# Rows of maxima of items 1, 3 and 4 sent through DRAM earlier on the sync queue, in a Trainium2 kernel of two layers

## What is computed

```python
x = L0_attn_u                                   # (1, 2048, 128)
x = x + _L0_attn_ref(_layernorm(x), ...)        # mixer
x = x + _L0_ffn_ref(_layernorm(x), ...)         # attention, experts
x = x + _L1_attn_ref(_layernorm(x), ...)        # selective scan
x = x + _L1_ffn_ref(_layernorm(x), ...)         # network
```

```python
scores = jnp.einsum('bqhd,bkhd->bhqk', q, k) / jnp.sqrt(jnp.float32(HEAD_DIM))
causal = jnp.tril(jnp.ones((S, S), bool))
scores = jnp.where(causal, scores, jnp.finfo(scores.dtype).min)
attn = jax.nn.softmax(scores, axis=-1)
out = jnp.einsum('bhqk,bkhd->bqhd', attn, v).reshape(B, S, D)
```

## Time and profile before

| | us |
|---|---|
| three runs | 1247.94, 1248.20, 1252.96 |
| median | 1248.2 |
| the profiled execution | 1252.22 |
| its span in the trace | 1249.9 |

### The profile page before, as it was taken

The page is one execution under the profiler, slowest core; times in us unless marked ns, Lnnn a source line. Parts: engine busy times, 40 slices in busy tenths (PEclk is TensorE's granted clock), DMA queues, the critical chain, the costliest instruction groups (busy, mean ns, idle before and its releaser), DMA issues.

```text
span 1249.9 us, 16003 instructions
## 1 busy us (share of the span) xinstructions
PE 1120.0 (90%) x5702; PEld 594.1 (48%) x5702; DVE 931.8 (75%) x1737; ACT 783.9 (63%) x1156; POOL 327.6 (26%) x271
## 2 busy tenths in 40 slices
PE   5889878888999999989999899999979789799998
PEld 2455554443333333333322288887633334357776
DVE  4788678857887888878864188887789999984432
ACT  4767632455655656656678898667758677455554
POOL 4233332210000000000012131210179788840000
PEclk9789889999998999999999999999989999899999
DMA  5211464345000000000000132211223222200000
GB/s 152 79 41 69 122 148 102 86 102 119 2 1 1 2 1 2 1 1 1 2 19 12 42 109 66 78 51 36 84 84 111 85 110 93 102 1 6 4 9 18
DMA packets 30623, 67.29 MB, mean 54 GB/s; under 512 B 3952, under 2 KB 16240, under 8 KB 28496
## 3 DMA queue, kind: packets, MB, share of 16 engines
q1 hardware_dynamic: 30544, 66.27, 18.5%
HBM read 57.47 MB, written 8.78 MB: 53 GB/s over the span
## 4 chain that ended last, share of the span: by engine, by line
PE 57%; DVE 14%; POOL 9%; issue 8%; ACT 7%; DMA 1%; SPq 0%; DVEq 0%; POOLq 0%; ACTq 0%
PE psum L1353 8%; PE psum L1238 8%; PE psum L405 7%; PE psum L407 7%; PE psum L406 7%; PE psum L1307 7%; POOL drive L2142 6%; DVE mx L1250 6%; DVE hst L2164 2%; ACT probs L1321 2%; PE psum L551 1%; PE psum L543 1%; PE psum L475 1%; PE psum L1956 1%; DMA m_rows<-mrow 1%
## 5 line engine op out<-in xcount | busy, mean ns | idle before, releaser
L1250 DVE TENSOR_REDUCE mx<-psum 128x1 f32<-128x512 f32 (+3 forms) x640 | 349.2, 603 | 64.8 <-PE psum L1238 35.2
L1321 ACT ACTIVATE probs<-psum 128x1024 f32<-128x1024 f32 (+1 forms) x320 | 283.6, 936 | 173.7 <-PE psum L1307 152.7
L1238 PE MATMUL psum<-kz,qa 128*128 128x512 bf16 (+3 forms) x640 | 199.3, 354 | 18.5 <-DVE mx L1250 12.8
L1307 PE MATMUL psum<-qa,kz 128*128 128x512 bf16 (+1 forms) x640 | 176.2, 363 | 7.8 <-DMA qa<-m_rows 4.4
L2142 POOL TENSOR_TENSOR drive<-du,b_bc 128x1024 f32<-128x1024 f32 x64 | 149.5, 2367 | 10.6 <-DVE hx_lo L675 9.1
L1353 PE MATMUL psum<-probs,v 128*32 128x512 f32 (+3 forms) x1280 | 150.8, 541 | 1.5 <-POOL probs L1332 1.4
L1238 PEld LDWEIGHTS psum<-kz,qa 128*128 128x128 bf16 x640 | 57.2, 97 | 180.5 <-DVE mx L1250 131.9
L2083 PE MATMUL psum<-hst,ident 128*128 128x512 f32 x256 | 120.3, 614 | 22.7 <-DVE u L2182 14.1
L1332 POOL TENSOR_SCALAR_AFFINE_SELECT probs<-probs 128x512 f32<-128x512 f32 x48 | 29.4, 637 | 361.1 <-ACT probs L1321 361.1
L2164 DVE TENSOR_TENSOR_SCAN hst<-psum,hlast,drive 128x512 f32<-128x512 f32 x96 | 115.2, 1261 | 8.7 <-ACT psum L2096 5.0
L675 DVE TENSOR_TENSOR hx_lo<-hid,hx_hi 128x1024 fp32r<-128x1024 f32 x64 | 81.4, 1276 | 33.9 <-ACT hx_hi L1679 29.8
(11 more groups left out here) (294 smaller groups left out, 1944.6 us busy)
## 6 DMA issues: line engine op xcount, KB each, us to landing
b_bc<-b_rows SPq DMA_DIRECT2D x16, 1024.0 KB, 4.7
cs_bc<-cs_rows SPq DMA_DIRECT2D x16, 512.0 KB, 4.8
gate_bc<-gate_rows SPq DMA_DIRECT2D x32, 256.0 KB, 3.1
qk_part_rows<-qk_parts SPq DMA_DIRECT2D x48, 128.0 KB, 2.3
ew_raw<-experts_dram SPq DMA_DIRECT2D x8, 512.0 KB, 3.6
qa<-qk_part_rows SPq DMA_DIRECT2D x16, 192.0 KB, 5.3
kz<-qk_part_rows SPq DMA_DIRECT2D x16, 192.0 KB, 5.8
fw_raw<-net_dram SPq DMA_DIRECT2D x11, 256.0 KB, 2.7
```

Source lines behind the costliest of these rows:

```text
L1238: ins = pe.matmul(out[:, 0:w], qa[:, b, h // 2, i * P:(i + 1) * P], key_rows(h, c)[:, 0:w], start=True, stop=not last, skip_group_check=True)
L1250: dve.tensor_reduce(mx[:, 4 * i + h % 4, c:c + 1], fill_bank("mx", k, n)[:, 0:w], AX.X, ALU.max).then_inc(S["mx_read"], 1)
L1307: ins = pe.matmul(out[:, lo:], key_rows(h, kt // TPB)[:, kt % TPB * P:(kt % TPB + 1) * P], qa[:, b, h // 2, lo:], start=True, stop=not dia ...
L1321: act.activation(probs[:, st % 2, hh, :, lo:], s_pair[n % 2][:, :, lo:], ACT.Exp, scale=SCALE).then_inc(S["p_done"], 1)
```

## The change

Two things are written anew. `store_sp` can send a part of its six groups (`parts`), and `prep_sp` uses this for block 2. The rows of item 1 go ahead of the loads of block 1, those of item 3 between the first group and the other five of block 2's stores, and those of item 4 ahead of the loads of block 2.

```diff
-        def store_sp(sp, b):
-            for n, done in enumerate(("qk_evac", "parts_mid", "parts_done")):
-                for j, rows in enumerate((Q_ROWS, K_ROWS)):
-                    sp.wait_ge(S[done], 2 * b + j + 1)
...
+        PART_DONE = ("qk_evac", "parts_mid", "parts_done")
+        PARTS = [(n, j) for n in range(3) for j in range(2)]
+
+        def store_sp(sp, b, parts=PARTS):
+            for n, j in parts:
+                rows = (Q_ROWS, K_ROWS)[j]
+                sp.wait_ge(S[PART_DONE[n]], 2 * b + j + 1)
...
             store_sp(sp, 1)
             mrow_sp(sp, 0)
+            mrow_sp(sp, 1)
             load_sp(sp, 1)
-            mrow_sp(sp, 1)
 
             sp.wait_ge(S["x_mixed"], NB)
             blank_sp(sp, 2)
             mrow_sp(sp, 2)
-            store_sp(sp, 2)
+            store_sp(sp, 2, PARTS[:1])
+            mrow_sp(sp, 3)
+            store_sp(sp, 2, PARTS[1:])
+            mrow_sp(sp, 4)
             load_sp(sp, 2)
-            mrow_sp(sp, 3)
-            mrow_sp(sp, 4)
             store_sp(sp, 3)
             blank_sp(sp, 3)
             mrow_sp(sp, 5)
```

More of the change, by code:

```diff
@@ L1044, in blank_sp @@
                              ).then_inc(first_loaded[b % 2], 16)
-        def store_sp(sp, b):
-            for n, done in enumerate(("qk_evac", "parts_mid", "parts_done")):
-                for j, rows in enumerate((Q_ROWS, K_ROWS)):
-                    sp.wait_ge(S[done], 2 * b + j + 1)
[L1050 to L1053, removed]
+        PART_DONE = ("qk_evac", "parts_mid", "parts_done")
[4 more added lines that the diff above has]
+                sp.wait_ge(S[PART_DONE[n]], 2 * b + j + 1)
+                for g in range(len(rows)):
+                    if rows[g] == n:
+                        sp.dma_start(part_dram[j, b, g].rearrange("e h t -> h e t"), qk_parts[:, j, n, :]
+                                     ).then_inc(S[("q_saved", "k_saved")[j]], 16)
         def load_sp(sp, b):
```

## The result

The changed kernel takes 1242.12 us (median of 18 runs, 1238.47 to 1246.48) against 1247.76 us before (18 runs, 1244.80 to 1252.98). The ratio is 0.9953, with a 95% interval of 0.9938 to 0.9967: 5.6 us less, and by the interval 4.1 to 7.7 us less. Its profiled execution took 1245.95 us (before: 1252.22).

The account below looks back on a forecast made before the run. The engines were taken to pace the kernel, TensorE being busy for 90%. Stall 4.4 plus clock 1.3 made 5.7 us, taken from the median of 1248.2 to give 1242.5 us; range 1240.6 to 1248.4.

Parts of the forecast that it names:

- The stall of 4.40 us goes.: Before item 3 in attention: TensorE no longer waits for the rows of maxima, which land by about 244; 4.4 us.
- What the moves cost: nothing.: On the sync queue: later load 1, load 2 and item 2's rows still arrive before they are needed; no cost.
- The clock's term.: Item 3's first step: without the stall TensorE's clock stays at 1.00, worth 1.3 us, between 1.0 and 1.7.
- The 5.7 us should reach the end whole.: From item 3 to the kernel's end: the full gain of 5.7 us is kept, as engines' semaphores release everything behind.
- Rival 1: In the kernel after the stall: one more slow clock stretch drops out, another 1.7 us, gain 7.4, 1240.8 us; chance 0.24.
- Rival 2: At item 3 and the next items: ScalarE and VectorE waits give back 2 to 4 us, 1245.5 us; chance 0.13.
- Rival 3: Whole kernel: only the higher group of runs has the stall, so the median gains nothing, 1248.2 us; chance 0.07.
- Rival 4: At item 4's first maximum: load 1 lands late and stops TensorE, 1254.4 us or more if slower; chance 0.04.

Follow-up runs that it names:

- e1: The changed kernel with the rows of items 1 and 4 back in their old places, so only item 3's go early: 1243.84 us, ratio 0.9951.
- e2: The kernel before with only item 1's rows moved ahead of load 1: 1248.55 us, ratio 1.0006.
- e3: The kernel before with item 3's rows moved after all twelve stores of block 2 and ahead of load 2: 1244.26 us, ratio 0.9964.
- e7: The kernel before with item 3's rows between the first and the last four transfers of load 2: 1241.48 us, ratio 0.9952.
- e4: The kernel before with 17 matmuls, results overwritten, in front of TensorE's wait before item 3: 1247.44 us, ratio 0.9992.
- e8: The changed kernel with load 1 behind the rows of item 2 as well: 1255.07 us, ratio 1.0058.
- e10: The changed kernel with overwritten matmuls in TensorE's waits for item 1's columns and in the tails of items 3, 7 and 11: 1237.46 us, ratio 0.9919.

## Why the prediction was right

- **Time and sign.** 1242.5 predicted, 1242.12 measured; a gain of 5.7 us against 5.6. That the two agree to 0.1 us is luck: the interval of the gain is 4.1 to 7.7 us, and the terms measured in the traces make 6.2, not 5.7.
- **The stall of 4.40 us goes.** It did (4.53 with the overlap). e1 and e2 show that it is item 3's move that does it, e3 that its place ahead of load 2 is enough, e7 that even the middle of load 2 is. In the change the reads go out at 240.15, some 22 us before the scores.
- **What the moves cost: nothing.** Item 1's reads at 212.1 (212.13), load 1 from 213.4 (213.48), item 3's save at 239 (238.84), load 2 from 258.9 (259.06), item 2's reads by 236 (232.55): each as worked out or within its bound, and no wait came of it.
- **The clock's term.** The mechanism was right, the size was off. I took 1.3 us, between 1.0 and 1.7. The 1.0 came from comparing with item 2's step of 6.40 us, which had a wait of 0.38 us in it and one more unit to reduce, so it was no measure of item 3's step. That step took 5.77 us, not the 6.4 that I gave as a sign. The term measured 1.64 in the change and 1.63 in e4, near the upper bound of 1.7. VectorE's part in that step, which was to lower the term, hid nothing.
- **"The 5.7 us should reach the end whole."** This step holds for the median, but not in the way it was put. In the trace the lead was 6.2, 4.5, 7.1 and 6.3 us in turn, as slow stretches came (294.1) and went (half of that at 396.6, and 550.2) behind the place of the change. I had allowed for 5 to 6 us throughout.
- **Rival 1** (one more slow stretch drops out) is what this pair of traces shows within attention: net of those that came and went, 3.4 us of slow clock more than the stall's own are gone, and attention is 7.13 us shorter, 0.96 more than the 6.17 at the place of the change. The rival had put 1.7 us on it, and 0.8 is lost again behind attention. Over all runs, the interval of 4.1 to 7.7 us holds both the forecast's 5.7 and this rival's 7.4, so the medians do not decide between them.
- **Rival 2** (another wait in the stall's place): ScalarE did pace the start, its first scores' evacuation beginning at 263.78 right behind the projection's. But the next steps gave nothing back: the lead at item 5's rows was still 6.17 us.
- **Rival 3** (the higher group of runs is the one with the stall) is wrong. Kernels without a stall spread about as widely, the changed one from 1238.5 to 1246.5. The spread goes with the granted clock: the changed kernel's runs at 0.975 to 0.977 lie between 1238.5 and 1242.2, those at 0.967 between 1245.7 and 1246.2.
- **Rival 4** (load 1 late) did not come, and the price was right in kind: in e8 TensorE waits for 9.89 us and attention is 10.6 us longer. In the median it is 13 us. The room in the changed kernel is 8.7 us by e8's figure, where I had found at least 4.4.

## What to carry to other kernels

On one queue, put the small transfer that an engine waits for ahead of the bulk whose first use is far off: what costs is how much of the bulk is in front of it, here 1.3 us with nothing, 4.8 us behind 0.75 MB and 7.8 us behind 1.5 MB. One call moved (e3) gave the same length of attention as the whole change, so find the late item first and move only that. A stall of TensorE is dearer than its length, as the slow clock behind it adds here 0.4 us for each microsecond at the lower level; where the wait can't be removed, matmuls into a bank that is overwritten next can keep the clock up: in e4 the wait was no longer for them (4.67 us, beside 4.40 and 4.83 where it was empty), and the step behind it 1.63 us shorter.

## What was not expected of the hardware

Pauses of about a microsecond each can go ahead of a fall of the clock. Before the slow stretch of 294.1 TensorE was busy for 2.15 of 4.10 us, with two waits of 0.99 and 0.88 us for VectorE in item 3's tail; before the one of 396.6 in the kernel before it was busy for 3.15 of 4.60 us, with waits of 0.85 and 0.87 us. e10, with these waits filled, has no slow stretch in attention. But the same pauses do not always bring one, as e1 shows, and what else decides stays open.

The times of one kernel spread by 8 us (changed kernel, 18 runs), and a good part goes with the clock: over these runs the time falls by about 0.6 us for each 0.001 of mean granted clock, which accounts for some 70% of the variance. That slow stretches coming and going are the cause fits the traces, but there is one trace for each kernel, and two for the changed one. So two kernels of this kind should be compared over many runs, or by a length inside the trace with its slow stretches counted beside it.
